# Normalising images 2 to 8 in slices beside the scan of the preceding image

## The reference, cut to what matters

```python
    return residual + gamma * h          # h = gelu output times a gate per image and channel
...
    xh = jnp.transpose(x, (0, 2, 3, 1))
    mu = xh.mean(-1, keepdims=True)
    var = xh.var(-1, keepdims=True)
    xn = (xh - mu) * jax.lax.rsqrt(var + 1e-05) * ln_g + ln_b
    x_seq = xn.reshape(B, H * W, C)
...
    out_fwd = _mamba(x_seq, *mparams)
    out_bwd = jnp.flip(_mamba(jnp.flip(x_seq, 1), *mparams), 1)
```

## Time and profile before

| | us |
|---|---|
| runs, median (lowest to highest) | 5625.2 (5623.45 to 5625.22) |
| profiled execution, its own time | 5622.07 |
| span of the profiled execution | 5620.2 |
| `normalise`, first load to last store issued | 463.2 to 613.1 |
| first scan instruction of VectorE | 672.6 |
| VectorE busy, 1000 to 5500 us | 4497.26 of 4500 |

### The profile page before, as it was taken

How to read it: one execution, slowest core, us unless ns; L and a number is a source line. 1 busy time by engine, 2 the same in 40 slices (tenths; PEclk the granted TensorE clock), 3 DMA queues, 4 the chain that set the end, 5 groups by cost and what they waited for, 6 DMA issues and landing times. The chain is left out here.

```text
span 5620.2 us, 74988 instructions
## 1 busy us (share of the span) xinstructions
PE 4417.3 (79%) x17412; PEld 1176.0 (21%) x17412; DVE 5265.8 (94%) x3821; ACT 3184.7 (57%) x5221; POOL 4899.0 (87%) x2361
## 2 busy tenths in 40 slices
PE   6878577778878787788887887878778887788887
PEld 4553111111111111111111111111111111111111
DVE  5556499999999999999999999999999999999997
ACT  2237455555555566555666555665555566655564
POOL 0020299999999999999999999999999999999998
PEclk9999776667777777777777777777777777777777
DMA  2238555556656556666656665666665665666666
GB/s 75 76 92 241 164 189 184 186 183 200 212 191 202 196 196 197 207 193 209 191 194 196 204 204 198 196 196 197 202 208 189 206 194 194 198 206 198 205 193 200
DMA packets 365955, 1062.74 MB, mean 189 GB/s; under 512 B 71396, under 2 KB 119926, under 8 KB 315340
## 3 DMA queue, kind: packets, MB, share of 16 engines
q1 hardware_dynamic: 355724, 1045.89, 57.8%
q10 hardware_dynamic: 8064, 14.16, 0.8%
q0 software_dynamic: 1984, 1.06, 0.1%
HBM read 849.20 MB, written 211.63 MB: 189 GB/s over the span
## 5 line engine op out<-in xcount | busy, mean ns | idle before, releaser
L1464 POOL TENSOR_TENSOR hc<-hring,c_rep 128x1024 f32<-128x1024 f32 x1541 | 3599.4, 2358 | 73.1 <-DVE hring L1419 69.6
L1419 DVE TENSOR_TENSOR_SCAN hring<-decay,carry,u_ps 128x1024 f32<-128x1024 f32 x1221 | 2833.8, 2346 | 0.0
L1170 PE MATMUL u_ps<-stack_b,w_spread 48*128 48x512 bf16 x2442 | 992.4, 495 | 1008.6 <-DVE hring L1419 1003.7
L1401 DVE TENSOR_TENSOR u_ps<-u_ps,u_rep 128x1024 f32<-128x1024 f32 x1221 | 1491.7, 1222 | 69.0 <-DMA u_rep<-u_scr 52.9
L1295 ACT ACTIVATE decay<-dt_rep,w_a 128x1024 f32<-128x1024 f32 x1222 | 1396.4, 1145 | 221.2 <-DVE hring L1419 208.1
L1188 PE MATMUL y_ps<-hc,w_gather 128*32 128x512 f32 x6144 | 1131.2, 818 | 0.0
L1295 ACT ACTIVATE u_ps<-dt_rep,w_a 128x1024 f32<-128x1024 f32 x322 | 359.3, 1116 | 1104.2 <-DVE hring L1419 1103.9
L1451 POOL TENSOR_TENSOR drive_p<-u_rep,b_rep 128x1024 f32<-128x1024 f32 x322 | 759.5, 2359 | 10.7 <-DMA u_rep<-u_scr 10.7
L1419 DVE TENSOR_TENSOR_SCAN hring<-u_ps,carry,drive_p 128x1024 f32<-128x1024 f32 x321 | 755.7, 2354 | 0.0
L1170 PEld LDWEIGHTS u_ps<-stack_b,w_spread 48*128 48x128 bf16 x2442 | 144.8, 100 | 2371.0 <-DVE hring L1419 2166.7
L1211 PE MATMUL prep_ps<-xn,w_conv 128*128 128x512 f32 x792 | 476.6, 749 | 27.2 <-DMA xn<-xn_scr 25.5
(11 more groups left out here) (148 smaller groups left out, 4044.3 us busy)
## 6 DMA issues: line engine op xcount, KB each, us to landing
dt_rep<-dt_scr SPq DMA_DIRECT2D x194, 1024.0 KB, 5.9
u_rep<-u_scr SPq DMA_DIRECT2D x194, 1024.0 KB, 8.0
c_rep<-bc_scr SPq DMA_DIRECT2D x260, 512.0 KB, 4.9
b_rep<-bc_scr SPq DMA_DIRECT2D x130, 512.0 KB, 4.3
xn<-xn_scr SPq DMA_DIRECT2D x132, 384.0 KB, 5.4
y_scr<-y_sb SPq DMA_DIRECT2D x768, 64.0 KB, 2.0
xn<-xn_scr SPq DMA_DIRECT2D x132, 256.0 KB, 4.7
dt_scr<-dt_sb SPq DMA_DIRECT2D x260, 128.0 KB, 2.1
```

The lines of the kernel that those rows point to most:

```text
L1170: mm = nc.tensor.matmul(u_ps[nv % NSLOT][:, sl], w["spread"][:, q, :], upper(stack_b[drv][:, sl]), start=True, stop=True)
L1401: nc.vector.tensor_tensor(slot[:, :], slot[:, :], u_rep[r][:, b, :], ALU.mult).then_inc(drive_ready, 1)
L1419: nc.vector.tensor_tensor_scan(hring[nv % NHR][:, ::step], factor[:, ::step], term[:, ::step], carry[:, drv, nv:nv + 1], ALU.mult, ALU.add ...
L1464: nc.gpsimd.tensor_tensor(hc[nv % NHC][:, :], hring[nv % NHR][:, :], c_rep[q][:, :], ALU.mult).then_inc(c_applied, 1)
```

## The change

`normalise` keeps only image 1 (8 slices); `over_first` runs its stages over these. Images 2 to 8 are normalised in `scan`, one slice of 512 tokens in each of the first 56 of the 64 passes, by a new task `norm`. It works with tokens as rows. At step 5 SyncE's queue loads the slice of the gelu output, of x, and the gate column. At step 12 ScalarE scales the centring matrix by the gate; at 14 TensorE does 8 matmuls (4 blocks of 128 tokens, gelu output and x) into `prep_ps`; at 15 ScalarE squares with a sum along the row, at 16 it takes Ln and Exp of 4 columns and scales the 4 blocks; at 17 TensorE turns them back with 4 matmuls by the identity; at 18 ScalarE applies the affine part, and at 19 SyncE's queue stores.

So that `prep_ps` is free for this, the groups of the other tasks move to adjoining steps: `low` from step 2 to 1, `dt` from 4, 6, 8 to 3, 4, 5, `conv` from 14, 16, 18 to 18, 19, 20, the first z matmul from 20 to 21, the sums of y from 0 and 10 to 10 and 12, the projection from 12 to 13. Each step's evacuation by ScalarE stays one step later. The waits that order the uses of `prep_ps` follow. These new steps hold in all 64 passes, also in those that normalise nothing.

```diff
-        LOW_AT = 2
-        DT_AT = (4, 6, 8)
-        CONV_AT = ((14, 14, 14), (16, 16, 16), (18, 18, 18))
+        LOW_AT = 1
+        DT_AT = (3, 4, 5)
+        CONV_AT = ((18, 18, 18), (19, 19, 19), (20, 20, 20))
...
-        SLICE_AT, Z_AT = 15, (20, 22)
-        SUM_Y_AT, PROJECT_AT, RES_AT, OUT_STORE_AT = (0, 10), 12, 13, 14
+        SLICE_AT, Z_AT = 15, (21, 22)
+        SUM_Y_AT, PROJECT_AT, RES_AT, OUT_STORE_AT = (10, 12), 13, 14, 15
+        NORM_IN_AT, NORM_GATE_AT, CENTRE_AT, SQUARE_AT, SCALE_AT, TURN_AT, NORM_OUT_AT, NORM_STORE_AT = 5, 12, 14, 15, 16, 17, 18, 19
+        NORM_PASSES = 2 * (ITERS - CHUNKS)
...
+        def norm_slice(it, dr):
+            return it // CHUNKS + 1, it * 3 % CHUNKS * T + dr * SL
...
             with eng.Fori(0, CHUNKS - 1) as it:
-                iteration(it, (False, False), (False, False))
-            iteration(CHUNKS - 1, (False, True), (False, False))
-            with eng.Fori(CHUNKS, ITERS) as it:
-                iteration(it, (True, True), (True, True))
+                iteration(it, (False, False), (False, False), True)
+            iteration(CHUNKS - 1, (False, True), (False, False), True)
+            with eng.Fori(CHUNKS, ITERS - CHUNKS) as it:
+                iteration(it, (True, True), (True, True), True)
+            with eng.Fori(ITERS - CHUNKS, ITERS) as it:
+                iteration(it, (True, True), (True, True), False)
...  (SyncE)
+                def norm(m, p, it, dr, slicing):
+                    if m == NORM_IN_AT:
+                        image, at = norm_slice(it, dr)
+                        free, = ready(p + 1)
+                        sp.wait_ge(centred, free)
+                        sp.dma_start(gate_now[:, :], gate_all[:, bass.ds(image, 1)]).then_inc(norm_in, 16)
+                        sp.dma_start(nh[:, :], d["act_scr"][image, :, bass.ds(at, SL)]).then_inc(norm_in, 16)
+                        sp.dma_start(nx[:, :], d["x_tok"][image, :, bass.ds(at, SL)]).then_inc(norm_in, 16)
+                    if m == NORM_STORE_AT:
+                        image, at = norm_slice(it, dr)
+                        made, = ready(p + 1)
+                        sp.wait_ge(norm_out, made)
+                        sp.dma_start(d["xn_scr"][image, :, bass.ds(at + HALO, SL)], nout[:, :]).then_inc(norm_stored, 16)
...  (TensorE)
                             wait(pe, prep_out, NPREP * pn + g, not isinstance(pn, int) or pn + g > 0)
-                            if g == 0 and slicing:
+                            if g == 0 and beside[1]:
+                                pe.wait_ge(norm_out, pn - 1)
+                            elif g == 0 and beside[0]:
                                 pe.wait_ge(res_ready, pn - 1 - OUT_LAG)
...
+                def norm(m, p, it, dr, slicing):
+                    if m == CENTRE_AT:
+                        pe.wait_ge(norm_in, 48 * (p + 1))
+                        pe.wait_ge(centrer_gated, p + 1)
+                        if slicing:
+                            pe.wait_ge(res_ready, p - OUT_LAG + 1)
+                        else:
+                            pe.wait_ge(prep_out, NPREP * (p + 2))
+                        for j in range(NBLK):
+                            to, tok = prep_ps[:, j * C:(j + 1) * C], slice(j * P, (j + 1) * P)
+                            nc.tensor.matmul(to, nh[:, tok], gated_centrer[:, :], start=True, stop=False)
+                            mm = nc.tensor.matmul(to, nx[:, tok], w["centrer"][:, :], start=False, stop=True)
+                        mm.then_inc(centred, 1)
+                    if m == TURN_AT:
+                        pe.wait_ge(tokens_scaled, p + 1)
+                        for j in range(NBLK):
+                            mm = nc.tensor.matmul(prep_ps[0:C, j * P:(j + 1) * P], ntok[:, j, :], w["ident"][:, :], start=True, stop=True)
+                        mm.then_inc(turned_back, 1)
...  (ScalarE)
+                def norm(m, p, it, dr, slicing):
+                    if m == NORM_GATE_AT:
+                        act.wait_ge(norm_in, 48 * (p + 1))
+                        act.wait_ge(centred, p + 1)
+                        nc.scalar.activation(gated_centrer[:, :], w["centrer"][:, :], ACT.Copy, scale=gate_now[:, 0:1]).then_inc(centrer_gated, 1)
+                    if m == SQUARE_AT:
+                        act.wait_ge(turned_back, p + 1)
+                        act.wait_ge(centred, p + 2)
+                        for j in range(NBLK):
+                            mm = nc.scalar.activation(ntok[:, j, :], prep_ps[:, j * C:(j + 1) * C], ACT.Square, accum_out=nstat[:, 0, j:j + 1])
+                        mm.then_inc(norm_step, 1)
+                    if m == SCALE_AT:
+                        act.wait_ge(norm_step, 3 * p + 1)
+                        nc.scalar.activation(nstat[:, 1, :], nstat[:, 0, :], ACT.Ln, bias=neps[:, 0:1], scale=1.0 / C).then_inc(norm_step, 1)
+                        act.wait_ge(norm_step, 3 * p + 2)
+                        nc.scalar.activation(nstat[:, 2, :], nstat[:, 1, :], ACT.Exp, scale=-0.5).then_inc(norm_step, 1)
+                        act.wait_ge(norm_step, 3 * p + 3)
+                        for j in range(NBLK):
+                            mm = nc.scalar.activation(ntok[:, j, :], prep_ps[:, j * C:(j + 1) * C], ACT.Copy, scale=nstat[:, 2, j:j + 1])
+                        mm.then_inc(tokens_scaled, 1)
+                    if m == NORM_OUT_AT:
+                        act.wait_ge(turned_back, p + 2)
+                        act.wait_ge(norm_stored, 16 * (p + 1))
+                        nc.scalar.activation(nout[:, :], prep_ps[0:C, :], ACT.Identity, bias=w["lng"][:, 1:2], scale=w["lng"][:, 0:1]).then_inc(norm_out, 1)
```

More of the change, by code:

```diff
@@ L100, in over_slices, with over_first @@
     image(B - 1, last=True)
+def over_first(eng, *stages):
+    most = max(lead for lead, _ in stages)
+    for s in range(-most, NS):
+        for lead, what in stages:
+            if 0 <= s + lead < NS:
+                what(0, s + lead)
 def over_last(eng, *stages):
@@ L1022, in front, with conv @@
                         load_u(*later(4, u, n, it, dr))
-                def conv(m, pn, it, dr, slicing):
+                def conv(m, pn, it, dr, beside):
                     if m == XN_AT:
+                        counts = (16 * (pn - 1) if beside[1] else 16 * (NORM_PASSES + 1), NPREP * (pn - 1) + 3)
+                        stored, done = ready(*counts)
                         it = it if isinstance(it, int) else it % ITERS
-                        wait(sp, prep_done, NPREP * (pn - 1) + 3, not isinstance(pn, int) or pn > 0)
+                        wait(sp, prep_done, done, not isinstance(pn, int) or pn > 0)
+                        wait(sp, norm_stored, stored, not isinstance(pn, int) or pn > 1)
                         for tap, lo, hi, j, at in TAP_ROWS:
@@ L1275, in slice_out @@
                         mm.then_inc(projected, 1)
-                run(pe, ("front", front), ("back", back), ("prep", prep), ("slice", slice_out), ("conv", conv), ("gate", gate))
+                def norm(m, p, it, dr, slicing):
[16 more added lines that the diff above has]
+                        mm.then_inc(turned_back, 1)
+                run(pe, ("front", front), ("back", back), ("prep", prep), ("slice", slice_out), ("norm", norm), ("conv", conv), ("gate", gate))
             @block.scalar
@@ L1377, in slice_out @@
                         nc.scalar.copy(res[:, :], prep_ps[0:C, :]).then_inc(res_ready, 1)
+                def norm(m, p, it, dr, slicing):
[22 more added lines that the diff above has]
+                        nc.scalar.activation(nout[:, :], prep_ps[0:C, :], ACT.Identity, bias=w["lng"][:, 1:2], scale=w["lng"][:, 0:1]).then_inc(norm_out, 1)
                 act.wait_ge(zeroed, 1)
                 load_exp_ln(nc)
-                run(act, ("back", back), ("prep", prep), ("slice", slice_out), ("conv", conv), ("gate", gate), ("front", front))
+                run(act, ("back", back), ("prep", prep), ("slice", slice_out), ("norm", norm), ("conv", conv), ("gate", gate), ("front", front))
             @block.vector
@@ L1626, in vision_mixer_kernel @@
                 pointwise(nc, d, hs, gate, w)
-            normalise(nc, d, gate)
-        scan(nc, d, w)
+            normalise(nc, d, gate, w)
+            scan(nc, d, w, gate)
     output(nc, d)
```

74 lines of the change are left out of this document (49 added, 25 removed).

## The result

The changed kernel takes 5821.8 us (5814.27 to 5822.95, 4 runs) against 5625.15 us (5623.45 to 5625.22): a ratio of 1.0349, interval 1.0333 to 1.0364. It is slower by 3.5%. The sign and the mechanism were forecast; the size was not: 5821.8 lies above the range of 5530 to 5780.

What follows compares the result with a forecast made beforehand. VectorE was taken to bound the scan, each late spread costing its full time: 5622.1 - 118.3 (removed stage) + 122 (steps 18 to 20) + 45 (smaller places) = 5671, so 5674 us; range 5530 to 5780, the forecast's own 5631 to 5745.

Steps and rivals of the forecast that it cites:

- the three smaller places: Step 1, steps 4 to 6 and steps 12 to 14: late spreads, 0.7 us a pass together, 45 us.
- steps 18 to 20: TensorE's fullest stretch, all 64 passes: spread of step 20 late by 1.9 us a pass at low clock, 122 us.
- The places: Late spreads were expected ahead of VectorE's drives in steps 2, 6, 14 and 20.
- What is removed: 56 of 64 slices leave `normalise`, at 2.11 us each by its stores: 118.3 us less.
- Costs taken as nothing: ScalarE's added 3.6 us a pass, SyncE's 4 more issues and the added transfers: all covered, 0 us.
- Centring and turn: TensorE's added matmuls: 2.4 us a pass for centring at step 14, 1.1 for turning back at step 17.
- the formula: Steps 17 to 20: lateness is half the time run at low clock, less 0.7 us of slack; 1.4 to 4.7 us.
- the early rise: The clock rising 4.2 us, not 10.7, after TensorE starts running without a pause at step 17; lateness then 1.4 us.
- steps 4 to 6: `dt` group 2 waits for ScalarE behind a GpSimd unit's decay; spread of step 6 is 0 to 1.5 us late.
- steps 12 to 14: VectorE's second product ends a step before the projection; spread of step 14 is 0 to 1.1 us late.
- Rival 3: Late clock rise everywhere: 4.7 + 0.7 us a pass, 5853 us; chance 0.11.
- Rival 1: TensorE's clock stays high and steps 18 to 20 fit: 5507 us, or 5539 with 0.5 us a pass; chance 0.18.

Runs made afterwards that it cites:

- the filled pause: The changed kernel with the spread of step 15 issued twice and that of step 16 five times, same values rewritten; 5700.94 us, ratio 1.0129.
- the dt edit: The changed kernel with ScalarE evacuating each dt group in the step of its matmul, not one step later; 5667.16 us, ratio 1.0068.

## Why the prediction was wrong in size

Two terms of the sum were too small: the three smaller places, 0.7 us a pass where the runs showed 2.0, and steps 18 to 20, 1.9 us where they showed 2.7. In both, the bounds that the working gave held what was measured, and the figure taken lay too near to their lower end.

- *VectorE bounds the scan, and a late spread costs its full time*: right. 314 us of waits and 319 us of longer scan.
- *The places*: right, all four. Besides them only step 21 waited, 12 us in all.
- *What is removed*: 118.3 taken, 129.7 measured. I took the pace of one slice times 56, which leaves 14.8 us from the first store of the short stage to the last; it was 11.1 (472.3 to 483.4). The end of the stage is faster than its mean pace: before, the first eight stores took 14.9 us (480.1 to 495.0) and the last eight 11.7 (601.4 to 613.1). And the first load began 8 us earlier (455.6). That last part is not the stage's own: the stages ahead of it, whose steps are the same in both kernels, ended that much sooner. The first load stands at 454 to 456 us in all seven kernels with the short stage and at 463 to 465 in the five with the long one; no run shows why.
- *Costs taken as nothing* (ScalarE, SyncE's queue, the transfers): right for the normalisation's own work, as VectorE waited for none of them. But ScalarE held TensorE up ahead of step 6, by the old task `dt` at its new steps.
- *Centring and turn*: the halves took 0.11 us each at the high clock (8 centrings in 1.8 us, turn in 0.95), below my 2.4 and 1.1.
- *Steps 18 to 20*: the mechanism was right, the size failed. The count at the high clock was right (8.7 us in 8.83; the filled pause shows it), and the formula, half of the time run low less 0.7 us of slack, came near. In one pass 9.1 us low gave 3.4 us (formula 3.9); in the pass at 3049.81 it was 3.4 us low and the wait 1.2 (formula 1.0). Over the 64 passes the formula adds up to 194 us, and 173 were measured. I had the bounds, 1.4 to 4.7 us, and took 1.9, "nearer the early rise, since a late TensorE has no pauses and rises sooner". The early rise came in a part of the passes only: of the 64, 24 waited 1.3 to 1.9 us and 40 waited 2.8 to 3.5; the mean is 2.7. 64 x 2.7 = 173 us, where I had 122.
- *The three smaller places*: this term failed by more. 0.7 us a pass taken, 45 us; measured 6 + 85 + 38 = 129 us, or 2.0 a pass: 84 us too little, against 51 at step 20. For steps 4 to 6 my bound was 0 to 1.5 and it was 1.3 in every pass. I had written that ScalarE stands behind the decay there and that the low clock is the usual level there, and still took a low figure for all three, on the ground that these stretches hold fewer pauses. The clock did not rise for it: of the 8 us ahead of the drive of step 6 it was low for 7.5 or more in every pass. For steps 12 to 14 I had VectorE's second product done a step before the projection; in the trace TensorE waits 0.93 us for it in each of the 56 passes that have a projection, and 48 of these are late at step 14.
- *The sum*: 167 us of waits taken, 314 measured; 147 more, less 11 from the stage, is 136 of the 148 us by which the forecast fell short; the other 12 are the growth of the scan beyond its waits (319 against 314), of the gap before it (2.6) and the 4 us between the profiled executions and the medians. Rival 3 (5853) was the nearest, with 0.11, but only in number: it had 4.7 us in steps 18 to 20 and 0.7 elsewhere, and the runs showed 2.7 and 2.0. The range was too narrow for bounds that were worked out and then left.
- *Rival 1* (the clock stays high, on time) is what the filled pause makes happen at step 20 in 48 of the 64 passes, but only there.
- *The Trainium skill*, "TensorE: Matmul & The Clock Gate", Part 2, says that matmuls stay in program order: the trace agrees. VectorE waited 3.36 us for the spread of 3226.94, which began only at the end of conv group 2 (3224.17, 2.84 us).

A pass falls into the 3.4 or the 1.3 us case by how long the clock stays low behind the pause. What stays open is why it stays low for 9.1 us in most passes and for 3.4 in others, and how much of the side gain at steps 14 and 20 from the dt edit is clock.

## What to carry to other kernels

When an engine that is not the bound feeds the one that is, through an in-order queue, count for each feed the time from its release to its deadline, at the low clock as well, and treat what stands between as the budget. Work that moves from a stage of its own into such a queue may cost nothing (here 0 to 36 us for 56 slices), while moving its neighbours together to make room cost 340. If the work does not fit at the low clock, take the low figure for the sum unless a row shows that the clock is high just there. Look also for places where the queue must wait for another engine's evacuation, since the work behind such a wait has both less time and, here, the low clock.

## What the runs showed of the hardware

More work for TensorE made the kernel faster: 10 needless matmuls a pass, 8 of them in a pause of 2.6 us (the row of ten, 2.42 us, against 0.62 us for its own two), kept the granted clock at 1.00 for 30.6 us in the pass shown and took 139 us off one place. The pause that cost the clock was short, 2.55 us behind a stretch in which TensorE had been busy in part (5.10 of 6.80 us).
